# Batches 2 and 3 kept with each chunk backwards, and y without the quarter blocks above the diagonal

## The reference, cut to what matters

```python
A_dt = (dt * A).reshape(b, nc, CHUNK, H).transpose(0, 3, 1, 2)
A_cum = jnp.cumsum(A_dt, axis=-1)
L = jnp.exp(_segsum(A_dt))                       # lower triangular in (l, s)
Y_diag = jnp.einsum('bzlhn,bzshn,bhzls,bzshp->bzlhp', Cc, Bc, L, xch)
...
Y_off = jnp.einsum('bzlhn,bzhpn,bhzl->bzlhp', Cc, prev, jnp.exp(A_cum))
Y = (Y_diag + Y_off).reshape(b, s, H, P) + hs * D[None, None, :, None]
y = Y.reshape(b, s, INTER)
g = y * jax.nn.silu(gate)
```

## Time and profile before

| | us |
|---|---|
| median of the runs | 1763.0 |
| the profiled execution, its own time | 1765.28 |
| its span | 1763.4 |
| PE busy | 1722.1 (98%) |
| VectorE busy | 1265.6 (72%) |
| GpSimd busy | 1203.9 (68%) |
| ScalarE busy | 845.5 (48%) |
| y matmuls (L984), busy | 169.6 + 99.6 |

### The profile page before, as it was taken

One profiled execution on the slowest core, in us unless ns is written; L12 is line 12 of the kernel. 1 busy time (PEld: TensorE's weight loads), 2 busy tenths in 40 slices (PEclk: granted clock), 3 DMA queues, 4 the chain that ended last, 5 costly groups with the idle time before them and its releaser, 6 DMA issues. The chain is left out here.

```text
span 1763.4 us, 34371 instructions
## 1 busy us (share of the span) xinstructions
PE 1722.1 (98%) x10392; PEld 1412.2 (80%) x10392; DVE 1265.6 (72%) x1892; ACT 845.5 (48%) x1273; POOL 1203.9 (68%) x873
## 2 busy tenths in 40 slices
PE   6899999999999999999999999999999998999998
PEld 5688888888888888888888888888888886788886
DVE  7898648873888288728883788468846886877776
ACT  3666346643664266435652665356535652222221
POOL 3499659965897589757985799469956987524430
PEclk9999999999999999999999999999999999999998
DMA  3333012311231023103220232013201311111101
GB/s 101 88 89 91 25 49 84 86 35 37 84 91 42 30 79 91 54 18 89 80 67 18 72 91 72 18 61 91 85 18 57 84 50 61 49 36 49 48 13 48
DMA packets 71344, 107.23 MB, mean 61 GB/s; under 512 B 16743, under 2 KB 25063, under 8 KB 71307
## 3 DMA queue, kind: packets, MB, share of 16 engines
q1 hardware_dynamic: 70296, 105.38, 20.2%
q10 hardware_dynamic: 1008, 1.38, 0.2%
HBM read 103.51 MB, written 3.15 MB: 60 GB/s over the span
## 5 line engine op out<-in xcount | busy, mean ns | idle before, releaser
L822 PE MATMUL proj<-xhi,w_hi 128*128 128x512 f32 x1072 | 432.9, 404 | 8.0 <-DVE gate L1167 8.0
L824 PE MATMUL proj<-xhi,w_lo 128*128 128x512 f32 x1072 | 419.8, 392 | 0.0
L823 PE MATMUL proj<-xlo,w_hi 128*128 128x512 f32 x1072 | 419.5, 391 | 0.0
L470 POOL TENSOR_TENSOR g_lo<-gated,g_hi 128x512 fp32r<-128x512 f32 x128 | 166.8, 1306 | 184.7 <-ACT g_hi L703 184.6
L1148 DVE SCALAR_TENSOR_TENSOR v<-proj,par_sb,v 128x510 f32<-128x510 f32 x378 | 275.0, 741 | 20.8 <-DVE v L1148 9.7
L822 PEld LDWEIGHTS proj<-xhi,w_hi 128*128 128x128 f32 x1072 | 201.9, 188 | 67.3 <-DVE gate L1167 14.6
L487 POOL TENSOR_TENSOR gated<-hs,gate 128x512 f32 (+1 forms) x128 | 191.0, 1514 | 71.8 <-DVE hs L1273 71.8
L824 PEld LDWEIGHTS proj<-xhi,w_lo 128*128 128x128 f32 x1072 | 201.9, 188 | 43.2
L823 PEld LDWEIGHTS proj<-xlo,w_hi 128*128 128x128 f32 x1072 | 202.2, 189 | 38.0
L434 POOL TENSOR_TENSOR w_lo<-w_raw,w_hi 128x512 fp32r<-128x512 f32 x144 | 182.5, 1287 | 64.2 <-ACT w_hi L583 64.2
L607 ACT ACTIVATE v<-proj,par_sb 128x512 f32<-128x512 f32 x126 | 98.1, 779 | 243.4 <-PE proj L824 243.4
(11 more groups left out here) (185 smaller groups left out, 3343.4 us busy)
## 6 DMA issues: line engine op xcount, KB each, us to landing
w_raw<-in_win SPq DMA_DIRECT2D x144, 256.0 KB, 2.7
fade_l<-faded SPq DMA_DIRECT2D x128, 256.0 KB, 3.3
wo_raw<-in_wout SPq DMA_DIRECT2D x64, 256.0 KB, 2.6
M<-in_w SPq DMA_DIRECT2D x14, 512.0 KB, 3.8
row_r<-rows SPq DMA_DIRECT2D x256, 3.0 KB
row_l<-rows SPq DMA_DIRECT2D x256, 3.0 KB
cb<-in_w SPq DMA_DIRECT2D x7, 512.0 KB, 3.4
out<-resid SPq DMA_DIRECT2D x8, 256.0 KB, 2.0
```

The lines of the kernel that those rows point to most:

```text
L470: e.tensor_tensor(g_lo[:, i % 2, :, :], gated[:, 4 * kk:4 * kk + 4, t * P:(t + 1) * P], g_hi[:, i % 2, :, :].bitcast(F32), ALU.subtract).t ...
L822: e.matmul(o, hi_l, hi_r, start=first, stop=False)
L823: e.matmul(o, hi_l, lo_r, start=False, stop=False)
L824: return e.matmul(o, lo_l, hi_r, start=False, stop=last)
```

## The change

Batches 2 and 3 (half h = 1 of every tile) are kept with the 128 tokens of each chunk in reverse order from the silu on; the tiles are written that way by the instructions that made them before (`turned_round`, a view with step -1), and read back forwards where the outputs are cut (`tokens`) and where squares are added. Two more triangles (`sums[1]`, `after_back`) give the sums and the mask for reversed chunks, and `upto`, now only the mask, is bf16. In a reversed chunk the zero block is the mirrored one: there the first 64 output columns need all 128 rows and the last 64 only the upper 64 rows, where a forward chunk's first 64 columns need only the lower 64.

`y()` now does the xfade products first (8 matmuls, as before), then for each chunk the 64 output columns that need all 128 rows (16 matmuls of 64 columns), then the 64 that need 64 rows only, for a forward and a reversed batch in turn (16 matmuls of 64 rows and 64 columns, four different quarters of the array one after another). Both banks are handed over (`yready`) at the end.

```diff
-        after, bias_bc, nega_bc = [sq[:, i * P:(i + 1) * P] for i in range(3)]
+        after, bias_bc, nega_bc, after_back = [sq[:, i * P:(i + 1) * P] for i in range(4)]
+        sums = [hs[:, 1, i * P:(i + 1) * P] for i in range(2)]
-        upto = sb("upto", [P, P])
+        upto = sb("upto", [P, 2, P], BF16)
...
+        def turned_round(ap, h):
+            ap = ap.rearrange("p (c l) -> p c l", l=P)
+            return ap[:, :, ::-1] if h else ap
...
+        def tokens(t, kk):
+            ap = gated[:, 4 * kk:4 * kk + 4, t * P:(t + 1) * P]
+            return ap[:, :, ::-1] if t >= TT // 2 else ap
...
+            e.affine_select(out=sums[1], in_=sums[1], compare_op=ALU.is_ge, fill=0.0,
+                            base=0, pattern=[[-1, P]], channel_multiplier=1).then_inc(s_sums, 1)
+            e.memset(after_back, 1.0).then_inc(s_sums, 1)
+            pool.wait_ge(s_sums, 2)
+            e.affine_select(out=after_back, in_=after_back, compare_op=ALU.is_gt, fill=0.0,
+                            base=0, pattern=[[1, P]], channel_multiplier=-1).then_inc(s_sums, 1)
+            pool.wait_ge(s_const, 6)
+            e.tensor_copy(upto[:, :, :], hs[:, 1, 0:2 * P].rearrange("p (z l) -> p z l", z=2)).then_inc(s_sums, 1)
...
-                e.tensor_tensor(g_lo[:, i % 2, :, :], gated[:, 4 * kk:4 * kk + 4, t * P:(t + 1) * P],
-                                g_hi[:, i % 2, :, :].bitcast(F32), ALU.subtract).then_inc(glo.sem, 1)
+                e.tensor_tensor(g_lo[:, i % 2, :, :], tokens(t, kk), g_hi[:, i % 2, :, :].bitcast(F32), ALU.subtract)\
...
-                    e.tensor_tensor(halves(sqacc, h), halves(sqacc, h), sq[:, :], ALU.add)\
+                    total = turned_round(halves(sqacc, h), 0)
+                    e.tensor_tensor(total, total, turned_round(sq[:, :], h), ALU.add)\
...
-                e.activation(halves(dst, h), v[:, h, :], ACT.Tanh).then_inc(tanh.sem, 1)
+                e.activation(turned_round(halves(dst, h), 0), turned_round(v[:, h, :], h), ACT.Tanh)\
+                    .then_inc(tanh.sem, 1)
...
             for c in range(TT):
                 mm = e.matmul(ybank[c // 4][:, (c % 4) * P:(c % 4 + 1) * P], dta[:, c * P:(c + 1) * P],
-                              upto[:, :], start=True, stop=True)
+                              sums[c // 4], start=True, stop=True)
...
+                    def block(b, z, head, rows, part, inputs, slot, start, stop):
+                        first, width = part
+                        at = (b % 2) * S + z * P + first
+                        return e.matmul(ybank[b // 2][head * HD:(head + 1) * HD, at:at + width],
+                                        inputs[rows, head * HD:(head + 1) * HD],
+                                        M[rows, slot + head, b * P + first:b * P + first + width],
+                                        start=start, stop=stop)
+                    every, whole, low, high = slice(0, P), (0, P), (0, HD), (HD, HD)
                     for b in range(B):
-                        cols = slice(b * P, (b + 1) * P)
-                        for z, part, slot, inputs in ((0, 0, 0, xdt[:, 2 * b, :]), (1, 0, 4, xfade[:, b, :]),
-                                                      (1, 1, 2, xdt[:, 2 * b + 1, :])):
+                        for head in range(2):
+                            block(b, 1, head, every, whole, xfade[:, b, :], 4, not b % 2, False)
+                    for b in range(B):
+                        for z in range(2):
                             for head in range(2):
-                                mm = e.matmul(
-                                    ybank[b // 2][head * HD:(head + 1) * HD,
-                                                  (b % 2) * S + z * P:(b % 2) * S + (z + 1) * P],
-                                    inputs[:, head * HD:(head + 1) * HD], M[:, slot + head, cols],
-                                    start=(part == 0), stop=(part == z))
-                        if b % 2:
-                            mm.then_inc(yready.sem, 1)
+                                block(b, z, head, every, (high, low)[b // 2], xdt[:, 2 * b + z, :], 2 * z, False, False)
+                    for b in range(B // 2):
+                        for z in range(2):
+                            final = b == 1 and z == 1
+                            for other in range(2):
+                                for head in range(2):
+                                    mm = block(b + 2 * other, z, head, slice(other * HD, (other + 1) * HD),
+                                               (low, high)[other], xdt[:, 2 * (b + 2 * other) + z, :], 2 * z,
+                                               False, final)
+                                if final:
+                                    mm.then_inc(yready.sem, 1)
...
-                e.scalar_tensor_tensor(halves(dst, h), halves(dst, h), 1.0, v[:, h, :], ALU.add, ALU.mult)\
+                kept = turned_round(halves(dst, h), 0)
+                e.scalar_tensor_tensor(kept, kept, 1.0, turned_round(v[:, h, :], h), ALU.add, ALU.mult)\
```

More of the change, by code:

```diff
@@ L193, in mamba_ffn @@
         s_marks = sem("batch_marks_copied")
+        s_sums = sem("sums_made")
         s_wdt_split = sem("wdt_split")
@@ L391, in _ @@
             e.memset(ident[:, :], 0.0).then_inc(s_const, 1)
-            e.memset(upto[:, :], 1.0).then_inc(s_const, 1)
+            e.memset(hs[:, 1, 0:2 * P], 1.0).then_inc(s_const, 1)
             e.memset(after, 1.0).then_inc(s_const, 1)
@@ L397, in _ @@
                             base=0, pattern=[[-1, P]], channel_multiplier=1).then_inc(s_const, 1)
-            e.affine_select(out=upto[:, :], in_=upto[:, :], compare_op=ALU.is_ge, fill=0.0,
+            e.affine_select(out=sums[0], in_=sums[0], compare_op=ALU.is_ge, fill=0.0,
                             base=0, pattern=[[1, P]], channel_multiplier=-1).then_inc(s_const, 1)
@@ L469, in lower @@
                 pool.wait_ge(gused.sem, gused.window(g, i - 1))
-                e.tensor_tensor(g_lo[:, i % 2, :, :], gated[:, 4 * kk:4 * kk + 4, t * P:(t + 1) * P],
-                                g_hi[:, i % 2, :, :].bitcast(F32), ALU.subtract).then_inc(glo.sem, 1)
+                e.tensor_tensor(g_lo[:, i % 2, :, :], tokens(t, kk), g_hi[:, i % 2, :, :].bitcast(F32), ALU.subtract)\
+                    .then_inc(glo.sem, 1)
             def step(g, j, par_, nxt, nxt2, ahead):
@@ L597, in _ @@
                 act.wait_ge(s_dtp, h + 1)
-                e.copy(halves(dt_heads, h), ybank[h][:, :]).then_inc(s_dtc, 1)
+                e.copy(turned_round(halves(dt_heads, h), 0), turned_round(ybank[h][:, :], h)).then_inc(s_dtc, 1)
             def tap3(h, weights, nready, vfree, banks=proj):
@@ L617, in hs_tanh @@
                 act.wait_ge(taken.sem, ntaken)
-                e.activation(halves(dst, h), v[:, h, :], ACT.Tanh).then_inc(tanh.sem, 1)
+                e.activation(turned_round(halves(dst, h), 0), turned_round(v[:, h, :], h), ACT.Tanh)\
+                    .then_inc(tanh.sem, 1)
             def gate_tanh(dst, h, nready, banks=proj):
                 act.wait_ge(ready.sem, nready)
-                e.activation(halves(dst, h), banks[h][:, :], ACT.Tanh, scale=0.5).then_inc(tanh.sem, 1)
+                e.activation(turned_round(halves(dst, h), 0), turned_round(banks[h][:, :], h), ACT.Tanh, scale=0.5)\
+                    .then_inc(tanh.sem, 1)
             act.wait_ge(s_dtv, 2)
@@ L702, in g_upper @@
                 act.wait_ge(glo.sem, glo.window(g, i - 1))
-                e.copy(g_hi[:, i % 2, :, :], gated[:, 4 * kk:4 * kk + 4, t * P:(t + 1) * P]).then_inc(ghi.sem, 1)
+                e.copy(g_hi[:, i % 2, :, :], tokens(t, kk)).then_inc(ghi.sem, 1)
             def step(g, j, par_, nxt, nxt2, ahead):
@@ L887, in _ @@
             pe.wait_ge(s_dta, 1)
+            pe.wait_ge(s_sums, 3)
             for c in range(TT):
                 mm = e.matmul(ybank[c // 4][:, (c % 4) * P:(c % 4 + 1) * P], dta[:, c * P:(c + 1) * P],
-                              upto[:, :], start=True, stop=True)
+                              sums[c // 4], start=True, stop=True)
             mm.then_inc(s_cum, 1)
             for b in range(B):
-                mm = e.matmul(misc[:, b * P:(b + 1) * P], after, dta[:, 2 * b * P:(2 * b + 1) * P],
+                mm = e.matmul(misc[:, b * P:(b + 1) * P], after if b < B // 2 else after_back, dta[:, 2 * b * P:(2 * b + 1) * P],
                               start=True, stop=True)
@@ L1166, in gate_silu @@
                 dve.wait_ge(tanh.sem, ntanh)
-                e.scalar_tensor_tensor(halves(dst, h), halves(dst, h), 1.0, banks[h][:, :], ALU.add, ALU.mult)\
+                kept = turned_round(halves(dst, h), 0)
+                e.scalar_tensor_tensor(kept, kept, 1.0, turned_round(banks[h][:, :], h), ALU.add, ALU.mult)\
                     .then_inc(taken.sem, 1)
@@ L1216, in cbs_kept @@
                 dve.wait_ge(cbr.sem, ncb)
-                mask = upto[:, :].unsqueeze(1).broadcast_to([P, B, P])
```

(6 more changed lines are left out.)

## The result

| | median of 4 | lowest to highest |
|---|---|---|
| before | 1764.16 us | 1761.17 to 1765.62 |
| after | 1784.44 us | 1782.86 to 1787.95 |

After is slower: ratio 1.0122 [1.0105, 1.0139], where 1746 us was forecast. The profiled execution took 1785.35 us, its span is 1783.2.

What follows compares the result with a forecast made beforehand. PE was taken to bound the kernel, with a GpSimd and VectorE cycle close under it; 1765.3 - 14.7 (y) - 4.5 (long step) + 1.3 (cycle) = 1747.4, about 1745 against the median, stated as 1746 us, range 1740 to 1774.

Steps and rivals of the forecast that it cites:

- y's matmuls, after: PE's new y: 40 matmuls, 80 records, priced at 2.54 us against 2.78, 0.23 less.
- y, 0.23 us less: The shorter y on PE, over 64 y's: 14.7 us gained if PE's path is the end of each step.
- The long step goes: 4.5 us: The step of 15.67 us in each group of eight was to go: 8 x 0.56 = 4.5 us gained.
- The cycle takes back 1.3 us: GpSimd and VectorE wait on each other with period 14.98 us, close under PE's; charged 1.3 us in all.
- Reversed views free: VectorE, ScalarE and GpSimd reading one half per tile with step -1 was taken to cost zero.
- rival R: Reversed reads dearer on GpSimd, its two-input instruction +0.47 us, the kernel 1776 us; chance 0.09.
- The later hand-over: yready for y's first bank comes some 1.2 us later; forecast to cost nothing, with 1.7 us of cover.
- the work before the loops: Four added GpSimd instructions before the first root, about 1.4 us, forecast to cost nothing under 1.89 of cover.
- D: Rival: GpSimd and VectorE's cycle keeps the long step at 15.67 us, six others 14.98; 1755 us, chance 0.13.
- Q: Rival: y's quarters run only two at a time, y 3.00 us; the kernel 1773 us, chance 0.07.
- N: Rival: a narrow record costs as much as a wide one, y 3.78 us; 1823 us, chance 0.04.
- The sequencer's 62 ns a matmul: Skill's rule for software decoding on PE: 80 records take 4.96 us, kernel some 1900; one chance in a hundred.

Runs made afterwards that it cites:

- e2: The changed kernel with PE's loop over groups written out, its inner loop kept; 1747.87 us, 0.9923 of before.
- e11: e2 run again, beside e9 and e10; 1749.74 us, 0.9913 of before.
- e10: The kernel before, its y and loops untouched, with both squares of the gated tile moved from GpSimd to ScalarE; 1754.72 us, 0.9937 of before.
- e9: As e2, with both squares of the gated tile moved from GpSimd to ScalarE; 1743.14 us, 0.9875 of before.
- e8: As e2, with only the first half's square of the gated tile moved from GpSimd to ScalarE; 1753.18 us, 0.9933 of before.
- e1: The changed kernel's reversed layout, constants and bf16 mask, but y with its 24 matmuls of 128 columns as before; 1763.36 us, 1.0001 of before.
- e7: As e2, but y's last 16 matmuls of 64 columns on all 128 rows instead of 64; 1765.88 us, 1.0012 of before.
- e4: The kernel before with PE's loop over groups written out; 1762.81 us, 1.0000 of before.
- e3: The kernel before with two more steps written out in PE's group loop body, 123.6 KB instead of 94.7; 1800.57 us, 1.0220 of before.

## Why the prediction was wrong

**The step that failed is in the change part by part, "y's matmuls, after": it counted 80 records for 48 and priced them only as time on the array. That they are also instructions in the body of a loop, and what a jump back costs once the body doesn't stay loaded, has no term in the sum and is not among the rivals; it was put at nothing without a reason.** It is worth 36.5 us (e2 against after), more than all the rest together, and turned a gain into a loss. The trace of before held one half of it: its 19 fetches, none of them in the second to the seventh group, say that the body stayed loaded; and the change adds 16 matmuls, which are 32 records and 32 weight loads, to each of the body's four steps: 256 instructions of 64 bytes, 16 KB. What no row of before said is where the limit is, and before was 4 KB or less under it.

Without that, the forecast held: 1747.9 and 1749.7 us (e2, e11) for 1746. That it is so close is in part luck, for three terms were off by 1.4 to 3 us and two of these offset the third. By its terms:

- **y, 0.23 us less.** Measured 0.19: 2.78 to 2.58 by the rows above, 0.19 by the steps (15.113 to 14.927). Narrow pairs start 0.058 us apart (0.057 taken), the quarters in fours every 0.058 (0.058 taken), the four 7 ns apart. The change of layout inside y cost 0.15 as taken. The pieces came out 0.00, 0.02 and 0.02 us dearer (the wide pairs; the narrow ones with the change; the fours with the way out), and the terms of y before add up to 2.77, not to the 2.78 written, so nothing single was off by much. 64 x 0.19 = 12 us for 14.7.
- **The long step goes: 4.5 us.** It went, and a like hold in the interval with the window, which was not counted, went in part: 74.95 to 74.29 us in e2 is 0.66 less, 0.19 of it y's, so 0.47 x 7 = 3 us more than counted. The prediction had read from PE busy for 74.73 of 74.97 us that PE alone bounds that interval; e10, with PE's code untouched, takes 0.6 us out of it.
- **The cycle takes back 1.3 us.** In e2 the steps together are 2.7 us over 14.93 (2.3 in after): right in kind, too small. The many short waits for the gate that were forecast are there, on the weight loads (28 for 16). e9 shows it is the hold, by taking it away. e8 shows that the reason given for its size, GpSimd's period of 14.98, was not all: with a shorter chain on GpSimd the steps grew, to 7.6 us over. What counts is which GpSimd instruction is running when VectorE's hs arrives.
- **Reversed reads free.** Right (L527 1.287 us over all halves, 1.288 in e1), so rival R fell. One sign named for it could not tell: second halves of hs<-hs,v are longer than first ones in before too, because they wait out gated<-hs,gate. The later hand-over did not show: VectorE waits for y before its sum (L1320) once in the span, 2.8 us, where before it waits twice, 2.3. Nor did the work before the loops: the first y starts at 75.67 us, before 75.54.
- **Rivals.** D fell: no long step is left. Q fell: quarters go four at a time; e7 shows the step without them. N fell: pairs of 64 columns start every 0.058 us. The sequencer's 62 ns a matmul, which the prediction quotes for decoding in software, did not bind either: four records start in 58 ns. Which way instructions are decoded here no run shows.

Accounting: -12 (y) - 4.5 - 3 (holds) + 2.7 (cycle) + 36.5 (jumps) = +19.7; measured 1784.4 - 1764.2 = +20.3. Without the jumps it is -16.8; e2 measured 1747.9 - 1764.8 = -16.9.

## What to carry to other kernels

When an edit raises the number of instructions inside a loop, count the body in bytes before pricing the work, and look whether the instruction queue is silent while the loop runs: silent means that it stays loaded, and a body that grows past the edge loses some 6 us at every jump back (here from a size between 94.7 and 98.7 KB on PE). The cure is to write the outer loop out, since straight code is fetched without a stop (e2, e4); try that first, as one run. Taking work from an engine can place its next instruction under another engine's: look at what runs at the moment of arrival, not at the busy share.

## What the hardware showed that was not expected

- PE's loop body stays loaded or is fetched anew in every lap: no fetch of before falls between 227 and 1340 us at 94.7 KB, and nine packets a lap (16,384 bytes each, about 1 us of transfer) come at 98.7 to 110.7 KB, ten in e3 at 123.6. Why nine, where after's 110.7 KB fill seven, is open.
- Around a jump the packets came one by one, about 4 us apart (246.0, 250.2, 254.0 us): the first while PE still worked, the second while it stood (248.6 to 252.5). The clock fell to 0.50 at about that time, and the next eight to twelve matmuls at that level are nearly a third of the whole cost.
- VectorE's hs<-hs,v, with two inputs from SBUF, ends 0.55 us after a GpSimd instruction that runs when it starts; alone it takes 0.68. In before 120 of its 128 halves are held so, whichever of four GpSimd instructions they meet; nearly all of the second halves meet gated<-hs,gate in every kernel, e9 too.
- Four 64x64 blocks of the array run fp32 products at once, in 58 ns a set, the same as a pair of 128x64 blocks; entering that layout from the other costs 0.15 us: the first set starts 0.158 us after the last pair, and the second 0.107 after the first.
